# A routed-expert kernel: the pad writes move from one block ahead of slot 12 into the loop of slot loads

## The reference

```
h  = batchnorm(relu(patches(x) @ W.T + b))            # 16 x 746 tokens of 128
h += attention(layernorm(h)) @ Wo.T + bo              # 8 heads of 16, softmax over 746
e  = argmax(layernorm(h) @ Wr + br)                   # 8 experts, one for each token
h += gate * (relu(xn @ W1[e] + b1[e]) @ W2[e] + b2[e])  # 128 -> 512 -> 128, for the token's own expert
```

## Time and profile before

| | us |
|---|---|
| median of 3 runs (lowest to highest) | 1277.85 (1277.65 to 1279.09) |
| span of the profiled execution, first to last instruction | 1275.9 |
| median less span | 1.95 |
| first stage, up to the first transposition of a slot | 1048.46 |
| slots, from there to the end of the span | 227.4 |

### The profile page before, as it was taken

One profiled execution on the slowest core, in us unless ns is written; L12 is line 12 of the kernel. 1 busy time (PEld: TensorE's weight loads), 2 busy tenths in 40 slices (PEclk: granted clock), 3 DMA queues, 4 the chain that ended last, 5 costly groups with the idle time before them and its releaser, 6 DMA issues.

```text
span 1275.9 us, 53879 instructions
## 1 busy us (share of the span) xinstructions
PE 1178.7 (92%) x21379; PEld 745.5 (58%) x21379; DVE 1072.5 (84%) x2756; ACT 950.6 (75%) x2477; POOL 680.0 (53%) x894
## 2 busy tenths in 40 slices
PE   6479999999999999999999999999999846899996
PEld 3334656555555556555555556565644326899996
DVE  7469899999999999999999999999999544577774
ACT  4426988888887878788888878797877824567774
POOL 2062436566473837475665739374723334456664
PEclk9768999999999999999999999999999969899998
DMA  8152132222313131323223131313220513333331
GB/s 190 39 84 79 40 86 72 76 84 61 94 52 94 45 105 42 104 72 79 83 63 93 51 94 45 106 41 104 72 80 28 150 56 105 88 93 105 103 101 50
DMA packets 79409, 102.32 MB, mean 80 GB/s; under 512 B 15916, under 2 KB 72995, under 8 KB 78734
## 3 DMA queue, kind: packets, MB, share of 16 engines
q1 hardware_dynamic: 70624, 79.02, 23.4%
q0 software_dynamic: 8384, 20.22, 5.1%
q10 hardware_dynamic: 186, 0.02, 0.0%
HBM read 60.76 MB, written 38.93 MB: 78 GB/s over the span
## 4 chain that ended last, share of the span: by engine, by line
PE 63%; DVE 20%; issue 5%; POOL 3%; ACT 2%; DMA 1%; SPq 1%; another core or an unknown queue 1%; POOLq 0%; DVEq 0%; ACTq 0%
PE psum L1247 36%; DVE half_max L1112 14%; PE psum L1312 13%; PE psum L1391 6%; PE psum L1401 5%; PE psum L1252 2%; ACT arena L808 2%; DVE stats L916 1%; POOL out_dram L720 1%; DVE rows L990 1%; PE psum L1382 1%; POOL arena L405 1%; DMA arena<-max_rows 1%; PE psum L1267 1%; DVE arena L962 1%
## 5 line engine op out<-in xcount | busy, mean ns | idle before, releaser
L1112 DVE TENSOR_REDUCE half_max<-psum 128x1 f32<-128x373 f32 x1536 | 760.8, 534 | 62.8 <-PE psum L1247 55.0
L808 ACT ACTIVATE arena<-psum 128x373 f32<-128x373 f32 (+1 forms) x1536 | 655.0, 489 | 154.4 <-PE psum L1247 139.0
L1247 PE MATMUL psum<-k_rows,arena 96*32 96x373 bf16 x6144 | 519.1, 329 | 14.9 <-DVE half_max L1112 6.1
L1247 PE MATMUL psum<-arena,k_rows 98*32 98x373 bf16 x6144 | 515.7, 326 | 13.7 <-ACT arena L808 6.2
L1312 PE MATMUL psum<-arena,values 128*32 128x373 f32 (+1 forms) x3072 | 313.2, 478 | 0.2
L1247 PEld LDWEIGHTS psum<-k_rows,arena 96*32 96x32 bf16 x6144 | 173.8, 96 | 195.7 <-DVE half_max L1112 103.4
L1247 PEld LDWEIGHTS psum<-arena,k_rows 98*32 98x32 bf16 x6144 | 176.4, 95 | 178.2 <-ACT arena L808 74.8
L631 POOL DMA_INDIRECT routed_rows_dram<-rows,pos_i x96 | 96.6, 1007 | 170.7 <-PE psum L1247 106.2
L720 POOL DMA_INDIRECT out_dram<-arena,slot_id x101 | 119.2, 1180 | 90.0 <-issue 51.5
L1312 PEld LDWEIGHTS psum<-arena,values 128*32 128x32 f32 (+1 forms) x3072 | 98.4, 110 | 20.7 <-issue 2.8
L861 ACT COPY arena<-psum 128x128 f32<-128x128 f32 x101 | 26.9, 266 | 77.7 <-PE psum L1382 39.7
(11 more groups left out here) (218 smaller groups left out, 1447.5 us busy)
## 6 DMA issues: line engine op xcount, KB each, us to landing
arena<-q_parts_dram SPq DMA_DIRECT2D x192, 93.2 KB, 2.4
k_rows<-k_parts_dram SPq DMA_DIRECT2D x192, 93.2 KB, 2.4
arena<-routed_rows_dram SPq DMA_DIRECT2D x101, 130.0 KB
q_parts_dram<-q_part SPq DMA_DIRECT2D x48, 186.5 KB, 2.3
k_parts_dram<-k_part SPq DMA_DIRECT2D x48, 186.5 KB, 2.0
arena<-in_x_t_dram SPq DMA_DIRECT2D x3, 703.1 KB, 14.1
seq<-in_w_dram SPq DMA_DIRECT2D x1, 2048.0 KB
seq<-in_w_dram SPq DMA_DIRECT2D x8, 256.0 KB
```

The lines of the kernel that those rows point to most:

```text
L808: nc.scalar.activation(probs[0:kn(kt), G % N_P, j, :], st_bank[s % N_ST][0:kn(kt), 0:HALF], ACT.Exp).then_inc(s_exp, 1)
L1112: nc.vector.tensor_reduce(half_max[:, m:m + 1], mx_bank[m % N_MX][:, 0:HALF], AX.X, ALU.max)\
L1247: last = nc.tensor.matmul(dst[n:n + m], weights[:, n:n + m], moving, start=start, stop=stop)
```

## The change

The eight pads no longer stand in one block. SP waits for `s_tab` behind the load of slot 11. Then a loop over rounds 2 to 9 loads six slots (12 to 17, 18 to 23, and so on to 59) and issues one pad behind each round. A second loop loads slots 60 to 77. The waits for all scatters and all pads stand behind that loop, ahead of the late slots. Nothing changes on the other engines.

```
-    assert SLOTS <= 128
+    assert SLOTS <= 128 and 2 + E <= EARLY // ROUND
...
-        def pad_regions(engine, experts):
+        def pad_region(engine, e):
 
-            engine.wait_ge(s_tab, 1)
-            for e in experts:
-                first = engine.value_load(pad_i[0:1, e:e + 1], min_val=0, max_val=DEAD - D)
-                engine.dma_start(rows_dram[bass.ds(first, D), :], pad_row[:, :]).then_inc(s_pad, 16)
+            first = engine.value_load(pad_i[0:1, bass.ds(e, 1)], min_val=0, max_val=DEAD - D)
+            engine.dma_start(rows_dram[bass.ds(first, D), :], pad_row[:, :]).then_inc(s_pad, 16)
...
             for s in range(2 * ROUND):
                 load_slot(s, s % ROUND, s // ROUND)
-            pad_regions(sp, range(E))
-            sp.wait_ge(s_scat, B * NT * 16)
-            sp.wait_ge(s_pad, (E + 1) * 16)
-            with sp.Fori(2, EARLY // ROUND) as v:
+            sp.wait_ge(s_tab, 1)
+            with sp.Fori(2, 2 + E) as v:
+                for u in range(ROUND):
+                    load_slot(v * ROUND + u, u, v)
+                pad_region(sp, v - 2)
+            with sp.Fori(2 + E, EARLY // ROUND) as v:
                 for u in range(ROUND):
                     load_slot(v * ROUND + u, u, v)
+            sp.wait_ge(s_scat, B * NT * 16)
+            sp.wait_ge(s_pad, (E + 1) * 16)
             sp.wait_ge(s_tab, TABLES)
```

More of the change, by code:

```diff
@@ L567, in _ @@
                 load_slot(s, s % ROUND, s // ROUND)
-            pad_regions(sp, range(E))
+            sp.wait_ge(s_tab, 1)
[4 more added lines that the diff above has]
+            with sp.Fori(2 + E, EARLY // ROUND) as v:
+                for u in range(ROUND):
+                    load_slot(v * ROUND + u, u, v)
             sp.wait_ge(s_scat, B * NT * 16)
             sp.wait_ge(s_pad, (E + 1) * 16)
-            with sp.Fori(2, EARLY // ROUND) as v:
-                for u in range(ROUND):
-                    load_slot(v * ROUND + u, u, v)
             sp.wait_ge(s_tab, TABLES)
```

## The result

The changed kernel takes 1270.05 us (median of 5 runs, 1268.03 to 1272.82); the kernel before took 1277.85 in runs beside it (5 runs, 1274.92 to 1279.19). The ratio is 0.9945, with a 95% interval from 0.9931 to 0.9960: 7.0 us less, between 5.1 and 8.8. The forecast was 1270.2.

A forecast was written before the change was run, and what follows sets the result against it. PE alone was taken to set the even stretch at 1.90 us a slot, waiting before it at slot 12. 6.08 + 1.54 = 7.6 us off 1275.9 gives 1268.3, plus 1.95 for the median: 1270.2 us, range 1263.5 to 1274.3.

The forecast's parts named there:

- the register load ahead of each address: In SP's pad block: claimed to make SP's issuing larger than the landing wait, 8.34 us against 1.6 us.
- The load of slot 12 moves up: On SP: the load issued at 1082.15 can go at about 1073.8, its rows landing at about 1076.0.
- the 1.9 us that I had named as a sign: On PE's timeline: periods of 1.9 us from slot 11 on, with no gap at slot 12.
- The pause and the clock: On PE at slot 12: the 6.08 us gap goes and the slow clock behind it gives back 1.54 us.
- The pads in their new place: On SP, a pad behind each sixth load: 1.3 us each, next load 0.7 us late, hidden, cost nothing.
- the time to spare: Between a load's landing and PE's use in the even stretch: 1.80 us, which covers a late load.
- The moved waits and the second loop: Ahead of slot 78's load and at SP's added loop head: scatter and pad waits and the head cost nothing.
- A: Rival: PE's second pause, from 1107.80, goes too, 6.3 us more, giving 1263.9; chance 0.14.
- B: Rival: pads in the rounds set off late loads or pauses; two pauses give 1282.8, one 1276.5; chance 0.07.
- C: Rival: half is lost again, clock not given back (1271.8) or pads costing PE half a microsecond each (1274.2); chance 0.10.
- D: Rival: slot 12's pause stays, 1277.85, or only the landing's 1.6 us go, 1276.25; chance 0.04 and 0.01.
- E: Rival: SP waits for code fetch at the longer loop body or added loop head, up to 1282; chance 0.02.

## Why the prediction was right

*What bounded the kernel.* PE alone sets the slots of the even stretch, at 1.90 us each: it is busy for 56.00 of 56.00 us there, and those slots took the same with and without pads. The gap at slot 12 was SP's block of pads: it went with the block to slot 78, and it grew with the number of pads, from 0 (four) to 2.06 (six) and 4.25 us (eight). I had said that the register load ahead of each address makes SP's part the larger one. The profile does not bear this out: of the 1.1 us of a pad that load took 0.26 us (median of eight), the instruction that issues the DMA 0.33, and the register steps and the time between them the rest. SP's part was the larger because eight issues stood in a row ahead of one landing.

*The load of slot 12 moves up.* It was put at 1073.8 in the old profile, whose slots began 0.6 us later; it went at 1073.25. Right. The landing was taken as 2.17 us, and where PE waited for a load in the rounds it was 2.10 to 2.26. It can be shorter: 1.53 us were enough with four pads ahead. The period from slot 11 to 12 was not the 1.9 us that I had named as a sign, but 2.47, with a full clock and no wait for the rows; it is so in the kernels without the gap, from 2.12 to 2.47, and no term of the sum used it.

*The pause and the clock.* 6.08 + 1.54 = 7.6 us were forecast, and slots 11 to 23 gave 8.0: from slot 11 to 12 6.2, from 12 to 13 1.5, and 0.3 at slot 16, which I had not counted. The clock was given back whole. That it is tied to this wait, which I had only argued from the row beside it, is shown by four kernels: it fell behind the wait at slot 12 with eight and with six pads, moved to slot 78 with the block, and stayed full at slot 12 wherever PE did not wait for the rows.

*The pads in their new place.* Cost: nothing, and that held. The size of the term behind it was off. I had a pad at 1.3 us of SP's time and the next load 0.7 us late. In the loop the load behind a pad came 2.99 to 3.34 us after the one ahead of it, so it was 1.1 to 1.4 us late, nearly twice that. The pad's own steps were not the reason, 1.2 to 1.4 us against the 1.3 I had put; it was the way from the pad over the end of the loop to the next load, 1.6 to 2.1 us against the 1.3 between two loads. It still hid, since the time to spare was as I had it: 4.04 us less a landing of 2.1 to 2.26, that is 1.8 to 1.9. Behind one pad PE still started 2.6 us or more after its load's issue, so some 0.4 us were left. The experiment with two pads a round says that it tips between 1.4 and 2.45 us of lateness.

*The moved waits and the second loop.* No wait at slot 78, slots 77 to 84 took 13.3 us in both kernels. Right.

*The rivals.* A did not come: the second pause stayed, at 6.43 us from slot 23 to 24 where it was 6.50. A part of it did: slot 24 to 25 took 2.71 instead of 3.62 us, with the clock low for 3.4 us instead of 6.8. That is the 1.1 us that the slots gained beyond the forecast. I had said that nothing links this pause to the first. The profiles say that something does, for this small part: slots 23 to 28 took 16.0 us in the two kernels with a wait of 4.25 us or more at slot 12, and 14.0 to 14.9 in the nine others, among them the kernel before with its block moved to slot 78. How the one acts on the other is not shown. The low end of the range, 1263.5, is not what A's own sum gives, 1263.9; nothing hangs on it. B: no new pause appeared in any of the kernels with pads in the rounds. C fell with the clock and with slots 28 to 77. D fell with the two kernels whose waits or block were moved. E: SP's two loop heads and longer body cost PE nothing; the branch of the loop with the pads took 40 to 58 ns, as before.

*The sum.* The span fell by 9.7 us, more than the 7.6: 8.0 at slot 12, 1.1 at the second pause, 0.6 ahead of slot 0. The medians fell by 7.8. That the median agrees with the forecast to 0.2 us is luck in part: 1.1 + 0.6 us of the span's fall were in no term, and single runs lie 4.8 us apart here and up to 11.8 in the experiments (twelve runs of one kernel). The two profiles of the changed kernel differ by 3.8 us, of which 3.1 lie ahead of slot 0.

## What to carry to other kernels

A queue that issues loads has two budgets: its time in a round, and the lateness of one load. Work that fits the first easily can still break the second when it stands in one block; spread over rounds one pad of 130 KB a round was free here and two were not, and in one block four were free and six were not (five was not tried), where the queue's own idle time paid for a good part. Before such work is moved, compare one load's time from issue to use with its landing, and where a total scatters by some us, time the stage that was edited by an instruction that every turn has once.

## What was not expected of the hardware

- Behind a wait of PE of 2.06 us the granted clock fell to the level of 1.2 GHz for 3.4 us, and it cost 1.7 us more (3.58 us for a slot instead of 1.90). Waits of 4.25 and 8.64 us cost 1.5 us so, no more than the short one. A wait of 2.54 us in the same profile, some 20 us before, cost nothing of this kind. With the rounds of four engines written out the clock fell at 1064.6 us, behind a wait of 1.83. The length of the wait alone does not say whether the clock falls.
- The load behind a pad in the loop comes 1.6 to 2.1 us after the pad, where two loads in a row are 1.3 us apart. The pad itself is no dearer in the loop: the second of two pads there took 1.16 us (rows at slot 30), as one in the block does, although its place in `pad_i` comes from a register. The loop's end and head stand in this stretch; the kernel before has them too.
- Behind slot 23 ACT, DVE and PE stand for 3 to 4 us, on something that the trace calls remote for ACT and DVE, wherever the code of the loops lies. POOL does not: its store of slot 17 starts late, and three more follow it 1.3 to 1.4 us apart. The rows of the changed kernel (the first is that late store):

```profile
1097.59 1.10 POOL L722 DMA_INDIRECT out_dram<-arena,slot_id  x1 [2.69 <-issue]
...
1103.46 0.27 ACT L863 COPY arena<-psum 128x128 f32<-128x128 f32 x1 [4.35 <-remote]
1103.48 0.29 DVE L1211 TENSOR_TENSOR arena<-psum,seq 128x128 f32<-128x128 f32 x1 [3.25 <-remote]
```
